# Two-layer cross- and self-attention on one core: keys stored by feature tile, first rows asked for earlier, batch 1's value products and operand splits moved into the lead, GpSimd's loads issued sooner

## The reference, cut to what matters

```python
# x: (2, 512, 320)   ctx_768: (2, 1024, 192)
# layer 0
query = x @ Wq ; keyt = ctx[:, :-4] @ Wk ; valt = ctx[:, :-4] @ Wv
hs = mha(query, keyt, valt, 8 heads of 40)                  # softmax(q k^T d^-0.5) v
ca_q1 = einsum('btc,th->bch', ctx[:, -4:], Wq_ca)[:, indices]
ca_hs1 = mha(ca_q1, x, x) ; ca_q2 = ca_hs1 @ Wq
ca_hs2 = mha(ca_q2, ctx[:, -4:] @ Wk_ca, ctx[:, -4:] @ Wv_ca)
x = (hs + ca_hs2) @ Wout + b_out + x
# layer 1
x = attn(ln(x), ln(x), q1, k1, v1, o1, 20 heads of 16) + x
x = attn(ln(x), ctx, q2, k2, v2, o2, 20 heads of 16) + x
x = geglu(ln(x)) @ ff_w2 + ff_b2 + x
```

## Time and profile before

| | us |
|---|---|
| median of 3 runs | 925.62 (924.35 to 929.48) |
| profiled execution, its own time | 928.74 |
| its span from first to last instruction | 926.9 |
| matmuls busy in it | 851.4 |
| VectorE busy | 615.8 |
| ScalarE busy | 470.8 |

### The profile page before, as it was taken

How to read it: one execution, slowest core, us unless ns; L and a number is a source line. 1 busy time by engine, 2 the same in 40 slices (tenths; PEclk the granted TensorE clock), 3 DMA queues, 4 the chain that set the end, 5 groups by cost and what they waited for, 6 DMA issues and landing times.

```text
span 926.9 us, 11358 instructions
## 1 busy us (share of the span) xinstructions
PE 851.4 (92%) x4148; PEld 465.4 (50%) x4148; DVE 615.8 (66%) x1156; ACT 470.8 (51%) x682; POOL 82.1 (9%) x109
## 2 busy tenths in 40 slices
PE   4769989999999999999999789999999999799998
PEld 3646744444466576333334433333333332478988
DVE  4245547777683555799966587899999991756132
ACT  4523444445552441466675403667777679465030
POOL 3200000400004021000000300000000000130000
PEclk9977999999997998599999955999999999989999
DMA  6938668632302065122216230222222000600000
GB/s 219 273 113 238 195 179 261 179 97 85 101 19 65 0 197 175 48 68 68 62 28 111 74 108 1 53 53 53 53 52 53 1 2 2 240 1 1 29 1 29
DMA packets 30966, 83.18 MB, mean 90 GB/s; under 512 B 5172, under 2 KB 9212, under 8 KB 28606
## 3 DMA queue, kind: packets, MB, share of 16 engines
q1 hardware_dynamic: 30110, 79.71, 30.4%
q0 software_dynamic: 800, 2.73, 1.0%
HBM read 56.12 MB, written 25.89 MB: 88 GB/s over the span
## 4 chain that ended last, share of the span: by engine, by line
PE 60%; DVE 25%; DMA 7%; ACT 4%; issue 3%; POOL 1%; SPq 0%; DVEq 0%; ACTq 0%; POOLq 0%
PE PS L859 16%; PE PS L802 13%; DVE maxp L961 10%; PE PS L1390 8%; PE PS L553 8%; PE PS L839 6%; DVE negm L961 5%; PE PS L1402 4%; DMA k_d<-split 2%; DMA q_sl<-msplit 2%; PE PS L1200 2%; DMA ca_nat<-in_ca 2%; DVE turned L994 1%; ACT probs L925 1%; DVE stats L1243 1%
## 5 line engine op out<-in xcount | busy, mean ns | idle before, releaser
L925 ACT ACTIVATE probs<-PS 128x1024 f32<-128x1024 f32 (+1 forms) x336 | 311.7, 971 | 153.0 <-PE PS L839 147.4
L961 DVE TENSOR_REDUCE maxp<-PS 128x1 f32<-128x512 f32 x448 | 280.1, 679 | 49.9 <-PE PS L802 48.9
L802 PE MATMUL PS<-k_sl,q_sl 48*128 48x512 f32 (+3 forms) x640 | 264.1, 493 | 23.5 <-DMA q_sl<-q_d 11.1
L802 PEld LDWEIGHTS PS<-k_sl,q_sl 48*128 48x128 f32 (+2 forms) x640 | 120.2, 201 | 201.1 <-DVE maxp L961 121.2
L839 PE MATMUL PS<-q_sl,k_sl 50*128 50x512 f32 (+3 forms) x672 | 204.2, 434 | 9.4 <-ACT probs L925 5.2
L961 DVE TENSOR_REDUCE negm<-PS 128x1 f32<-128x512 f32 (+1 forms) x192 | 120.9, 679 | 28.1 <-PE PS L802 28.0
L839 PEld LDWEIGHTS PS<-q_sl,k_sl 50*128 50x128 f32 (+2 forms) x672 | 103.3, 192 | 57.2 <-ACT probs L925 24.6
L859 PE MATMUL PS<-probs,v2c 128*32 128x512 f32 x640 | 88.3, 622 | 1.0
L591 DVE TENSOR_TENSOR split<-PS,split 128x512 fp32r<-128x512 f32 (+3 forms) x54 | 34.9, 650 | 48.7 <-ACT split L568 48.5
L859 PE MATMUL PS<-probs,v0c 128*64 128x512 f32 (+1 forms) x256 | 62.9, 612 | 0.0
L568 ACT CAST split<-PS 128x512 fp32r<-128x512 f32 (+3 forms) x54 | 29.9, 553 | 56.0 <-PE PS L553 46.5
(11 more groups left out here) (180 smaller groups left out, 1005.4 us busy)
## 6 DMA issues: line engine op xcount, KB each, us to landing
k_d<-split SPq DMA_DIRECT2D x20, 512.0 KB, 3.5
q_d<-split SPq DMA_DIRECT2D x12, 512.0 KB, 3.2
k_sl<-k_d SPq DMA_DIRECT2D x8, 640.0 KB
k_sl<-k_d SPq DMA_DIRECT2D x40, 128.0 KB
q_sl<-q_d SPq DMA_DIRECT2D x40, 128.0 KB
k_sl<-k_d SPq DMA_DIRECT2D x20, 256.0 KB
w_raw<-in_ff_w SPq DMA_DIRECT2D x1, 3840.0 KB, 11.7
k_d<-split SPq DMA_DIRECT2D x10, 256.0 KB, 3.7
```

The source lines that it names most:

```text
L802: nc.tensor.matmul(PS[0:a.qt, SBANKS[k % 3], 0:cn], q_view(g)[f:f + a.rows, j // a.stack, q * a.qt:(q + 1) * a.qt], k_view(g)[f:f + a.rows ...
L925: nc.scalar.activation(probs[0:a.size[t], x % PRING, :, 0:a.nq], PS[0:a.size[t], 2 * (x % 2):2 * (x % 2) + 2, 0:a.nq], ACT.Exp, scale=a.sc ...
L961: nc.vector.tensor_reduce((maxp if nch > 1 else negm)[0:a.qt, g.turn, o:o + 1], PS[0:a.qt, SBANKS[k % 3], 0:a.chunks[c][1]], AX.X, ALU.max ...
```

## The change

- The keys' jobs of a batch run over feature tiles, and within each over the two halves of the tokens; before it was the other way about.
- Batch 1's value tiles (8 jobs "v") move from `first` to `second`, between its "s" jobs; `second` begins with batch 1's keys, and its queries come after them.
- The splits of `c1`, `x1`, `wk2`, `wv2` are cut up and put between jobs on ScalarE and VectorE.
- Rows of group 0 are asked for after the store of the seventh "s" job, with a wait for the first five stores only.
- GpSimd issues "f", then "d", as soon as the context and its weights are in.
- `Wq` gets its high part from VectorE and its low part from GpSimd, while ScalarE casts x.
- In a step of the lead the jobs come ahead of the two max-scores.
- The ring goes on from `first` into `second` without a wait for all of the stores.

```diff
-        "a": [(act_t[:, :, 0:SQ], ins["x_t"][:, :, 0:SQ]), (w_s0[:], ins["Wq"])],
+        "a": [(act_t[:, :, 0:SQ], ins["x_t"][:, :, 0:SQ])],
+        "q": [(w_s0[:], ins["Wq"])],
...
     def key_jobs(w, dst, b):
-        return [feat_job(...) for c in (0, 512) for m in range(KF)]
+        return [feat_job(...) for m in range(KF) for c in (0, 512)]
     def first_jobs():
-        return q0_jobs(0) + key_jobs(WK0, k0_d, 0) + value_jobs(WV0, 0, v0c, 0) + value_jobs(WV0, 0, v0c, 1)
+        return q0_jobs(0) + key_jobs(WK0, k0_d, 0) + value_jobs(WV0, 0, v0c, 0)
     def second_jobs():
-        split_jobs = q0_jobs(1) + key_jobs(WK0, k0_d, 1)
+        q_jobs, k_jobs = q0_jobs(1), key_jobs(WK0, k0_d, 1)
+        k_jobs[0]["needs"] = ("c1a", "c1b")
+        k_jobs[2]["prepare"] = ("x1a",)
+        k_jobs[4]["prepare"] = ("x1b",)
+        q_jobs[0]["needs"] = ("x1a", "x1b")
+        q_jobs[2]["prepare"] = ("wk2",)
...
+        split_jobs = k_jobs + q_jobs + ca_jobs + k2_jobs
+        whole_jobs = value_jobs(WV0, 0, v0c, 1)
...
     def sp_first(sp):
-        first.wait_stored(sp)
+        sp_projection(sp, first, first.jobs[:Q0_END + 4])
         sp.wait_ge(first_ones, 1)
+        first.wait_some_stored(sp, Q0_END + 2)
         sp_load(sp, st, 0)
+        sp_projection(sp, first, first.jobs[Q0_END + 4:])
         for x in range(A_MAIN.kt + 1):
             sp_projection(sp, second, share(second, x, st.lead))
+            if x == 0:
+                first.wait_stored(sp)
             if x in (0, 4):
                 sp_load(sp, st, 1 + x // 4)
...
         for x in range(st.lead):
-            maxima([x])
             if side is not None:
                 pe_projection(pe, side, share(side, x, st.lead))
+            maxima([x])
             flips([x])
...
             act.wait_ge(loaded_c, ALL_C)
-            first_in.act(act, "c0", "wk0", "wv0")
-            act_projection(act, first, first.jobs[:K0_END])
+            first_in.act(act, "c0a", "c0b", "wk0", "wv0")
+            act_projection(act, first, first.jobs[:Q0_END + 2])
             act.wait_ge(loaded_e, ALL_E)
-            first_in.act(act, "c1")
+            first_in.act(act, "c1a")
+            act_projection(act, first, first.jobs[Q0_END + 2:Q0_END + 4])
+            first_in.act(act, "c1b")
+            act_projection(act, first, first.jobs[Q0_END + 4:K0_END])
             act.wait_ge(pads_set, 1)
             act_projection(act, first, first.jobs[K0_END:])
-            act.wait_ge(loaded_f, ALL_F)
-            first_in.act(act, "x1", "wk2", "wv2")
-            first.wait_stored(act)
             act_attention(act, S_FIRST, side=second)
...
+            dve.wait_ge(loaded_q, ALL_Q)
+            nc.vector.tensor_copy(w_q_high[:], w_s0[:]).then_inc(wq_high, 1)
             dve.wait_ge(loaded_a, ALL_A)
-            first_in.dve(dve, "x0", "wq")
+            first_in.dve(dve, "x0a", "x0b")
...
-            pool.wait_ge(first.low, first.ns)
+            pool.wait_ge(wq_high, 1)
+            nc.gpsimd.tensor_tensor(w_s0_low[:], w_s0[:], w_q_high[:].bitcast(F32), ALU.subtract).then_inc(wq_low, 1)
+            pool.wait_ge(loaded_c, ALL_C)
+            for dst, part in loads["f"]:
+                pool.dma_start(dst, part).then_inc(loaded_f, 16)
             for dst, part in loads["d"]:
                 pool.dma_start(dst, part).then_inc(loaded_d, 16)
-            for dst, part in loads["f"]:
-                pool.dma_start(dst, part).then_inc(loaded_f, 16)
```

More of the change, by code:

```diff
@@ L354, in key_jobs @@
     def key_jobs(w, dst, b):
[L355 removed]
+        return [feat_job(w, ctx_tiles(b * SK + c, 512), m, b, c, 512, dst) for m in range(KF) for c in (0, 512)]
     def value_jobs(w, layer, dst, b):
@@ L453, in build, with __init__ @@
     class Projection:
-        def __init__(self, name, jobs, banks=(0, 1, 2, 3), vbanks=(4, 5)):
-            self.banks, self.vbanks = banks, vbanks
+        def __init__(self, name, jobs, banks=(0, 1, 2, 3), vbanks=(4, 5), follows=None):
+            self.banks, self.vbanks, self.follows = banks, vbanks, follows
+            self.shift = follows.ns % RING if follows else 0
             self.jobs, ns, nv, nm = [], 0, 0, 0
@@ L477, in __init__, with slot, wait_slot @@
             self.stored = [sem(f"{name}_stored{s}") for s in range(RING)]
+        def slot(self, i):
+            return (i + self.shift) % RING
         def wait_stored(self, eng):
-            for s in range(RING):
-                n = len(range(s, self.ns, RING))
-                if n:
-                    eng.wait_ge(self.stored[s], 16 * n)
+            self.wait_some_stored(eng, self.ns)
         def wait_some_stored(self, eng, n):
             for s in range(RING):
-                eng.wait_ge(self.stored[s], 16 * len(range(s, n, RING)))
+                times = sum(self.slot(i) == s for i in range(n))
+                if times:
+                    eng.wait_ge(self.stored[s], 16 * times)
+        def wait_slot(self, eng, i):
+            s = self.slot(i)
+            if i >= RING:
+                eng.wait_ge(self.stored[s], 16 * sum(self.slot(k) == s for k in range(i)))
+            elif self.follows:
+                eng.wait_ge(self.follows.stored[s], 16 * sum(self.follows.slot(k) == s for k in range(self.follows.ns)))
     first = Projection("first", first_jobs())
-    second = Projection("second", second_jobs(), (0, 1, 2), (3, OBANK))
+    second = Projection("second", second_jobs(), (0, 1, 2), (3, OBANK), first)
     selfp = Projection("selfp", self_jobs(), (2, 3, 6, 7))
@@ L510, in inputs_in @@
         if ph is first and j["at"] == 0:
-            first_in.wait(eng, "x0", "wq")
+            first_in.wait(eng, "x0a", "x0b")
+            eng.wait_ge(wq_low, 1)
         if ph is first and j["at"] == Q0_END:
-            first_in.wait(eng, "c0", "wk0")
+            first_in.wait(eng, "c0a", "c0b", "wk0")
         if ph is first and j["at"] == K0_END:
             first_in.wait(eng, "wv0")
-        if ph is first and j["at"] == V0_END:
-            first_in.wait(eng, "c1")
-        if ph is second and j["at"] == 0:
-            first_in.wait(eng, "x1", "wk2", "wv2")
-            eng.wait_ge(loaded_f, ALL_F)
-            eng.wait_ge(loaded_d, ALL_D)
+        if "needs" in j:
+            first_in.wait(eng, *j["needs"])
+        if "loaded" in j:
+            eng.wait_ge(*j["loaded"])
         if ph is selfp and j["at"] == 0:
@@ L1462, in _ @@
                 sp.dma_start(dst, part).then_inc(loaded_a, 16)
+            for dst, part in loads["q"]:
+                sp.dma_start(dst, part).then_inc(loaded_q, 16)
             for dst, part in loads["c"]:
@@ L1466, in _ @@
                 sp.dma_start(dst, part).then_inc(loaded_e, 16)
-            sp_projection(sp, first)
             sp_first(sp)
```

77 lines of the change are left out of this document (47 added, 30 removed).

## The result

| kernel | median, us | lowest to highest | runs |
| --- | --- | --- | --- |
| before | 926.07 | 924.35 to 929.48 | 5 |
| after | 919.70 | 917.64 to 922.61 | 5 |

A forecast was written before the change was run, and what follows sets the result against it. TensorE, busy 92%, bounds it through waits before the first Exp. 37.3 + 6.1 + 62.0 - 1.6 + 0.4 + 0.6 + 0.5 = 105.3 puts the Exp at 107.8, 13.7 us earlier: 925.6 - 13.7 = 912, range 905 to 918.

The forecast's parts named there:

- What bounds the kernel: Whole kernel: TensorE, busy 92%, bounds it; only its waits ahead of the first Exp can be won.
- The start: First product at 12.2 us against 12.11, as VectorE and GpSimd exclude each other; gain 0, upper end 1.6.
- The value tiles: End of `first`: fifth store lands at 29.8, third value tile starts at 31.0, `second` at 37.3 us.
- Group 0's rows: Before the first max-scores: rows in between 39.5 and 42.3, TensorE there at 41.1; wait 0 to 1.2, taken 0.6 us.
- the collision rival: Lead: first stores and rows run into each other, with later rows, ring wait and half clock; 918 us, chance 0.21.
- The spell in the small products: Small `ca` products of the lead: old half clock of 83.1 to 93.3 us kept inside the carried-over 62.0 us.
- The ring: Store slots in `second`: a store landing late behind group 1's rows costs 0.5 us, from 0 to 3.
- The loads: GpSimd's "f" and "d", issued from 12.6 us on, land by 33, so nothing waits for them.
- the rival by which the load is not what holds: Lead: "f" still lands near 50 and TensorE waits for `x1`; time within 0.5% of before, chance 0.06.
- the slower case: Lead: small products and rows' waits keep the clock low, up to 930 us; chance 0.02.
- The first rival: Lead: half clock of 83.1 to 93.3 and behind the value tiles goes too, 5.9 us more gained; 906, chance 0.19.

The follow-up runs named there:

- wq_low_by_dve: Changed kernel with Wq's high part cast by ScalarE and its low part subtracted by VectorE, not GpSimd: 917.08 us, ratio to the kernel before 0.9899.
- rows_asked_late: Changed kernel with group 0's rows asked for only after all nine first stores have landed, as before: 922.52 us, ratio to the kernel before 0.9966.
- d_after_rows: Changed kernel with GpSimd's list "d" loaded only after the first pair of max-scores: 918.54 us, ratio to the kernel before 0.9894.
- pairs_step_later: Changed kernel with each pair of max-scores one step later in the lead: 918.93 us, ratio to the kernel before 0.9898.
- spread_wq_dve: Changed kernel with the six small context-query products spread among second-layer key jobs, and Wq's parts made by ScalarE and VectorE: 912.96 us, ratio to before 0.9855.
- ca_spread: Changed kernel with the six small context-query products spread, one ahead of each two second-layer key jobs: 913.25 us, ratio to the kernel before 0.9856.
- ca_rows_apart: Changed kernel with the 24 products of eight columns moved behind batch 0's second-layer values: 920.26 us, ratio to the kernel before 0.9921.
- spread_rows_apart: Changed kernel with the six small products spread and the 24 of eight columns moved behind batch 0's second-layer values: 919.06 us, ratio to before 0.9913.
- before_ca_spread: Kernel before with only its six small context-query products spread among the second layer's key tiles: 927.79 us, ratio to the kernel before 1.0008.

## Why the prediction was wrong

- **What bounds the kernel; nothing behind the first Exp changes.** Right. 806.1 us in place of 805.4, inside the 7 us of scatter in the table.
- **The start, a gain of 0.** Right to 0.1 us (12.09 against 12.2), and by the mechanism given, though not in its order: GpSimd's subtraction was to come last, behind all of VectorE's. VectorE's first subtraction and GpSimd's ran in turn, VectorE first, in the other order than in the earlier trace rows, and then VectorE's second one waited for GpSimd's and was the last. The Trainium skill, SBUF — State Buffer, "Who interferes with whom", states this exclusion, and the trace agrees (2.58 in place of 0.69). wq_low_by_dve shows that this costs about 0.6 us. The cast's lower end of 0.5 was half of ScalarE's time and not half of its rate; it took the 0.80 that was forecast.
- **The value tiles.** The fifth store was taken to land at 29.8; the ninth cast ran at 30.38, and `second` started at 36.9 where 37.3 was forecast. The size is right. Its cause was placed wrong: I let the loads push the fifth store, while they pushed the very first one to 7.59 us, which moved casts five to nine together.
- **Group 0's rows: the first failed step.** "The wait is 0 to 1.2 us; I take 0.6." It was 3.1. TensorE was at the first pair at 40.9, as forecast (41.1); the rows came at 43.98 instead of 41.7. The request came 1.2 later than forecast, at 30.96, and the landing took 13.0, which is the far end that group 1's rows gave (12.5: 13.4 less 0.9 for a store), and not the mean that I took between it and a rate. rows_asked_late and d_after_rows show that the landing goes with the request (12.5 and 11.6 us behind it). The wait is 2.5 us longer than forecast; TensorE was 0.2 ahead, so 2.3 us of the miss. The rate of 228 GB/s, the near end, came from a stretch full of stores; in before from 44 to 48.7, when little but group 0's rows came in, it was 179 GB/s at a DMA share of 0.63 (the row stands below). That share is what ten busy engines of sixteen give. The prediction's 7.6 us took ten engines for the copies of 40 partitions only. The copies of 80 partitions read 40 rows as well, two parts of each; if they too go to ten, 6.3 us become 10.1, an estimate, and the rows are in at 43.3. No run shows the spread directly.
- **The clock behind that wait: a missing term.** In the forecast a gap of over 2 us with its spell stood only in the collision rival. 6 us at 0.51 are 2.9 us. The trace of before had such a spell, and I misread it. I put the half clock of 55.8 to 59 down to the idle gap just ahead of it, and took it out of the sum; but the clock had fallen at 48.7, inside the wait for rows (43.9 to 52.06), and stayed down. Stretches of before, columns as above:

```profile
44.00:48.70 4.70, 0.00 (x0) 0.00 (x0) 0.00 (x0) 0.38 (x2) 0.00 (x0) 1.00 0.63 179
48.70:55.80 7.10, 1.21 (x3) 0.53 (x3) 3.55 (x5) 2.73 (x3) 0.00 (x0) 0.50 0.17 47
```

In the kernels with the new order a spell of 6 to 7 us went with rows' waits of 3.1, 3.5 and 7.6, one of 3 us with 2.4, and none with 1.1 to 1.7 (five kernels), but none with 2.8 either. Two waits for a low part, near 25 us, were of one length, 3.29 in pairs_step_later and 3.28 in spread_wq_dve; a spell of 4 us followed the first and none the second. So the length of the wait is not all of it.

- **The spell in the small products: mis-sized.** The sum took the old stretch over with its half clock of 83.1 to 93.3 as it was. It became 67 to 84, 17.0 us at 0.50 in place of 10.2 at 0.51: 8.5 - 5.0 = 3.5 us more. That the order around small products decides its length is shown by ca_spread (3.5 us of spell, 4.9 of the 8.1 us of first Exp). That the 24 of eight columns start it is supported by ca_rows_apart, where the six small ones ran at full clock without them, and by the set: in all eleven kernels with the new order a fall came 0.1 to 5.3 us behind the first of the 24; in five of them an idle gap of 1.0 to 3.1 us stood there too. I had only weighed whether the spell goes or stays, not that the change, by putting the 24 and the six side by side, could lengthen it.
- **The ring, 0.5.** TensorE did not wait for it. ScalarE did, 2.48 at 58.39.
- **The loads.** "f" was in by 21.7, well before 33, as the forecast had it; the rival by which the load is not what holds is out.
- **The sum.** 2.3 + 2.9 + 3.5 - 0.5 = 8.2 of lateness, where 6.9 is seen; 1.3 is not traced to one place. The 2.3 already has in it that no half clock came in the value tiles (0.8 was forecast).
- **The rivals.** What happened is in part the collision (given 0.21) and in part the slower case's mechanism, that small products and a wait for rows keep the clock low. The collision's own terms add up to 1.5 + 1.5 + 2.5 + 1.2 = 6.7, which makes 919 and not 918. Its rows came as it says (42.3 + 1.5 = 43.8, measured 43.98), but its 2.5 for the ring did not come, and the 3.5 of the longer spell is not in it. That its sum lies next to the measured 919.7 is luck. The first rival (906) needs a first Exp at 101.9, and no kernel reached it: the best was 105.98.

What stays open is the rule by which a fall starts. In the kernel before, the same 24 products ran at 61 to 67 at full clock and the fall came 16 us later; a rule by the 24 alone is refuted by that. TensorE's timeline of before:

```profile
61.01 1.65 PE L1082 MATMUL PS<-ctx_last,w_kca 128*128 128x8 f32 x12
...
65.01 1.66 PE L1082 MATMUL PS<-ctx_last,w_vca 128*128 128x8 f32 x12
```

The two twelves stand 2.4 us apart there, with products of 512 columns between them, and 0.5 us apart in after, with two small ones between. All three kernels with the old order have that distance and no fall there; ca_rows_apart has 1.6 us and a fall, and spread_rows_apart 2.3, of which 1.0 is idle, and a fall. So their spacing is a candidate, and no run varied it alone. The Trainium skill, TensorE: Matmul & The Clock Gate, "HAM oscillation — how this bites in real kernels", explains falls by idle gaps. The spell of 43 to 50, which began inside a gap, agrees with that kind of cause, and the one of 67 to 84 does not: TensorE is busy in every us of 50 to 67 ahead of it. Each variant moved other waits as well, so the small products' own share is read from moving them (ca_spread, ca_rows_apart) and not in isolation; that was not tried.

## What to carry to other kernels

When a change takes a stall out of a stretch, read the granted clock of that stretch and of what the new order puts next to each other: here two spells of half clock took back almost half of the gain while the busy row said 93%. Before forecasting a transfer at a rate, look for the same transfer elsewhere in the trace and take its time from issue to landing; the far end that it gave, 12.5 us, was right here to 0.5 us. And loads issued sooner are not free because the DMA engines look idle: the first stores behind them pay, and what waits for a slot of the ring pays next. Last, a spell taken out of one place need not shorten the kernel: on the kernel before it went, and the time stayed (1.0008).

## What the runs showed of the hardware that was not expected

- TensorE's granted clock fell to 0.50 for 17 us with no idle gap ahead (67 to 84 in after), behind 24 products of eight columns and with small ones of four rows in its first 13 us; with the same work spread it fell for 3.5 us (ca_spread).
- Matmuls of 320 columns took 0.47 us each as recorded at half clock and 0.31 at full, a start every 0.27 and every 0.15 (before_ca_spread, at 101 and at 96 us).
- A subtraction of VectorE on 512 columns took 2.58 us beside GpSimd's 3.01, and 0.69 without it. In both orders of start seen here, the later one was the longer for it (GpSimd's 960 columns took 3.01, where 1024 took 2.34 in the earlier trace rows). VectorE's operation of 1.52 us in the earlier trace rows took 0.32 in other places of that trace.
- A store of 512 KB landed 7.59 us after issue with 2.7 MB of GpSimd's loads issued around it (12.7 to 19.0 us), and 4.72 with only list "f" of them (d_after_rows), where a store of before took 3.90.
- The same instructions behind the first Exp took 799.1 to 806.1 us in 14 executions, and the longest had the lowest clock (0.93 against 0.95).
